# A graph network kernel on one core: relation bias, edge items and layer statistics moved into neighbouring stages, 816 places for attention items instead of 848, extremes by TensorE

## The reference, cut to what matters

```
x = x + relations(layernorm(x))     # sum over edges of (x W[type])[src], by dst, * 0.5**0.5
                                    #   + h_bias + x loop_weight * 0.5**0.5
x = x + experts(layernorm(x))       # edge attention over 8192 places gives the gates: top 2 of 4,
                                    #   softmax; out += gate_e * (gelu(x W1_e + b1_e) W2_e + b2_e)
x = x + neighbours(layernorm(x))    # x W_self + mean over edges of maxk32(x W_neigh)[src], by dst
x = x + slices(layernorm(x))        # 8 heads, 64 slices: softmax of logits, tokens, attention
                                    #   between tokens, back to rows, W_out and b_out
```

## Time and profile before

| what | us |
| --- | --- |
| median of 3 runs | 6084.98 |
| lowest and highest | 6080.4 and 6094.47 |
| the profiled execution, its time | 6074.39 |
| its span | 6072.7 |

### The profile page before, as it was taken

The page is one execution under the profiler, slowest core; times in us unless marked ns, Lnnn a source line. Parts: engine busy times, 40 slices in busy tenths (PEclk is TensorE's granted clock), DMA queues, the critical chain, the costliest instruction groups (busy, mean ns, idle before and its releaser), DMA issues. The chain is left out here.

```text
span 6072.7 us, 74083 instructions
## 1 busy us (share of the span) xinstructions
PE 4259.9 (70%) x18413; PEld 3046.3 (50%) x18414; DVE 2604.2 (43%) x8618; ACT 1712.5 (28%) x3921; POOL 3332.0 (55%) x3370
## 2 busy tenths in 40 slices
PE   5888877645555554467777777756668888888498
PEld 2455446333333333445555555545246666666366
DVE  7655424333333332433333333334944443443682
ACT  3344330000000000123333333325365543443132
POOL 5777665666666665055555555551256666666121
PEclk9999998776667766577878888878889999999698
DMA  6444442433333333122222122216144444443001
GB/s 219 154 158 156 158 155 79 130 92 93 91 92 92 92 96 82 14 70 43 43 41 44 40 44 42 42 34 191 41 147 144 138 121 121 121 121 115 16 1 43
DMA packets 331160, 564.00 MB, mean 93 GB/s; under 512 B 75064, under 2 KB 231365, under 8 KB 324507
## 3 DMA queue, kind: packets, MB, share of 16 engines
q0 software_dynamic: 141088, 319.86, 19.9%
q1 hardware_dynamic: 189789, 240.92, 12.6%
HBM read 461.01 MB, written 99.50 MB: 92 GB/s over the span
## 5 line engine op out<-in xcount | busy, mean ns | idle before, releaser
L990 POOL DMA_INDIRECT e_ring<-table,erow x1040 | 990.1, 952 | 523.4 <-issue 267.2
L1290 PE MATMUL e_sums<-e_ring,e_onehot 128*128 128x257 f32 x2080 | 772.2, 518 | 626.6 <-issue 351.5
L2236 POOL DMA_INDIRECT t_source<-source_rows,t_index x848 | 804.3, 948 | 717.9 <-DVE t_parts L2319 476.5
L1401 POOL DMA_INDIRECT e_ring<-table,esrc x800 | 791.2, 989 | 424.2 <-issue 207.3
L1290 PEld LDWEIGHTS e_sums<-e_ring,e_onehot 128*128 128x128 f32 x2080 | 494.0, 257 | 889.9 <-issue 570.8
L585 POOL DMA_INDIRECT r_ring<-rows,esrc x528 | 584.4, 1107 | 239.8 <-issue 131.8
L2395 PE MATMUL t_out<-t_w,t_hidden 128*128 128x256 f32 x1600 | 526.8, 459 | 172.3 <-issue 166.8
L1477 PE MATMUL e_total<-e_loads,e_times 128*128 128x256 f32 x2176 | 577.4, 397 | 47.7 <-issue 36.9
L2395 PEld LDWEIGHTS t_out<-t_w,t_hidden 128*128 128x128 f32 x1600 | 345.6, 225 | 308.6 <-issue 263.1
L1477 PEld LDWEIGHTS e_total<-e_loads,e_times 128*128 128x128 f32 x2176 | 413.3, 198 | 138.6 <-issue 64.7
L1488 PE MATMUL e_sums<-e_ring,e_onehot 128*128 128x256 f32 x1600 | 432.8, 393 | 48.7 <-DMA e_ring<-table,esrc 31.6
(11 more groups left out here) (447 smaller groups left out, 6371.8 us busy)
## 6 DMA issues: line engine op xcount, KB each, us to landing
table<-r_stage SPq DMA_DIRECT2D x49, 1024.0 KB
e_loads<-table SPq DMA_DIRECT2D x384, 128.0 KB
t_near<-near_rows SPq DMA_DIRECT2D x106, 256.0 KB
m_outputs<-first_outputs SPq DMA_DIRECT2D x49, 512.0 KB, 4.9
first_outputs<-t_stage SPq DMA_DIRECT2D x96, 256.0 KB
e_ring<-table,erow POOLq DMA_INDIRECT x1040
t_source<-source_rows,t_index POOLq DMA_INDIRECT x848
e_ring<-table,esrc POOLq DMA_INDIRECT x800
```

The costliest lines, as they stand in the source:

```text
L990: eng.indirect_dma_start(ring[:, t % BODY, 0:D], None, table, bass.IndirectOffsetOnAxis(ap=b.erow[:, EARLY + t:EARLY + t + 1], axis=0)).th ...
L1290: eng.matmul(sums[g % SUMS][:, 0:ACCW], onehot[t % ONEHOTS][:, :], ring[:, t % BODY, :], start=(t % GROUP == 0), stop=(t % GROUP == GROUP ...
L1401: eng.indirect_dma_start(ring[:, t % BODY, :], None, table, bass.IndirectOffsetOnAxis(ap=b.esrc[:, FROM + t:FROM + t + 1], axis=0)).then_i ...
L2236: eng.indirect_dma_start(source[s][:, q, :], None, a.source_rows, bass.IndirectOffsetOnAxis(ap=index[s][:, q:q + 1], axis=0)).then_inc(gat ...
```

## The change

What it does, function by function:

- **relation_sums** also loads h_bias, by SP ahead of its waits, and DVE adds it to b.x in seven pieces of seven windows (lift), at tiles 520, 528 and so on.
- **add_relations, the second row_statistics and edge_items** are one stage, joined_items. Its DVE code goes between the items' steps and join (b.x += acc * 0.5**0.5 for seven windows) and tally (bn_stats of seven windows).
- **The items are packed**: their edges are counted from a window's first edge, not from a tile's, so an item may begin anywhere in the sorted list. For that the last tile of every window is gathered (edge), the edges in it are counted, the ends and the item counts per window are laid out by a second product and six scan steps, and nine gathers fetch 128 edges from any position (anywhere).
- **attention_inputs**: the extremes over partitions come from a transpose and a product on PE with a DVE maximum between, instead of POOL's reduction; the memset of extra moves here; the store of source_rows increments a.sourced and is not awaited. **far_peaks** keeps one memset and makes the iota only in the wide path; **attention_edges** waits for a.sourced before POOL's first gather.
- **attention_edges**: MAIN is 816, so 102 turns, the last four without dense work and unrolled; b1 and b2 are loaded ahead of the weights, and PE waits for the weights of expert e at its first turn.
- **blend**: PE takes three experts, DVE the fourth (gate) ahead of its addition.
- **sparse_table**: the third statistics are combined at its start; MATCH_REPLACE8 writes TAKEN; the mask of what was taken is made by ACT (hide, seven windows late) and multiplied by POOL (choose).
- **add_neighbours, the fourth row_statistics and slice_weights** are one stage, neighbours_and_weights: ACT scales acc by the share, window by window, DVE joins and counts in runs of seven windows.
- **slice_tokens** writes the softmax rows in a layout by window (f.soft), half of it in the memory of big; **slice_output** multiplies from there without a copy and has four banks.

```diff
-MAIN = -(-(GT * N // GSPACE + NW + 16) // TURN) * TURN
+MAIN = -(-(GT * N // GSPACE + NW // 2 + 10) // TURN) * TURN
...
+TAKEN = -2.0 ** 127
...
+STATED = 7
+def variances(eng, s, b, stats, work):     # the seven combining steps of row_statistics
...
 def relation_sums
+    bias_at = [TILES // 2 + GROUP * j for j in range(RUNS)]
+            eng.dma_start(bias[:, :], m["h_bias"].rearrange("(a d) -> a d", a=1).broadcast_to([P, D])).then_inc(offset, 16)
             eng.wait_ge(keyed, 32)
...
+            def lift(j):
+                eng.wait_ge(restored, 16)
+                eng.wait_ge(offset, 16)
+                eng.tensor_tensor(b.x[:, RUN * j:RUN * (j + 1), :], b.x[:, RUN * j:RUN * (j + 1), :],
+                                  bias[:, :].unsqueeze(1).broadcast_to([P, RUN, D]), ALU.add).then_inc(biased, 1)
...
+                if t in bias_at:
+                    lift(bias_at.index(t))
...
 def attention_inputs
-            eng.dma_start(a.source_rows.rearrange("(w p) c -> p w c", p=P), a.rows[:, :, :]).then_inc(stored, 16)
-            eng.wait_ge(stored, 16)
+            eng.dma_start(a.source_rows.rearrange("(w p) c -> p w c", p=P), a.rows[:, :, :]).then_inc(a.sourced, 16)
...
-            eng.wait_ge(bounded, 1)
-            eng.partition_all_reduce(extremes[:, :], bounds[:, :], P, RMAX).then_inc(reduced, 1)
-            eng.wait_ge(reduced, 1)
+            eng.memset(a.extra[:, :, :], 0.0).then_inc(emptied, 1)
+            eng.wait_ge(emptied, 1)
...
+            eng.wait_ge(bounded, 1)
+            eng.transpose(turned[0][0:2 * HEADS, 0:P], bounds[:, :], b.ident[:, :]).then_inc(reduced, 1)
+            eng.wait_ge(bounded, 2)
+            eng.matmul(turned[1][:, 0:2 * HEADS], b.ones[0:2 * HEADS, :], laid[:, :], start=True, stop=True).then_inc(reduced, 1)
...
 def joined_items (DVE)
+            def join(j):
+                run = b.x[:, RUN * j:RUN * (j + 1), :]
+                eng.scalar_tensor_tensor(run, b.acc[:, RUN * j:RUN * (j + 1), 0:D], 0.5 ** 0.5, run,
+                                         ALU.mult, ALU.add).then_inc(joined, 1)
+            def tally(j):
+                eng.wait_ge(joined, j + 1)
+                for w in range(RUN * j, RUN * (j + 1)):
+                    eng.bn_stats(stats[:, w, :], b.x[:, w, :]).then_inc(tallied, 1)
...
+            eng.tensor_copy(whole[:, :], counted[0:NW, 0:1]).then_inc(bounded, 1)
+            join(0)
+            eng.wait_ge(edged, 16)
...
+            for j in range(EARLIER):
+                join(j + 1)
+                tally(j)
             eng.wait_ge(gathered, 16 * GROUND)
...
+            for j in range(EARLIER, RUNS):
+                if j + 1 < RUNS:
+                    join(j + 1)
+                tally(j)
...
 def attention_edges
+                eng.dma_start(w1[:, e, :, :], m["W1"][e].rearrange("(k p) f -> p k f", p=P)).then_inc(loaded[e], 16)
+                eng.dma_start(w2[:, e, :, :], m["W2"][e].rearrange("(j p) d -> p j d", p=P)).then_inc(loaded[e], 16)
...
+                if first_turn(t, 1):
+                    eng.wait_ge(a.sourced, 16)
+                    eng.sem_inc(cleared, 1)
...
+                if first_turn(u, EXPERTS):
+                    eng.wait_ge(loaded[e], 32)
...
-            eng.wait_ge(loaded, LOADS)
+            eng.wait_ge(offset, 32)
...
 def blend
+    TURNED = EXPERTS - 1
-                for e in range(EXPERTS):
+                for e in range(TURNED):
...
+            def gate(w):
+                eng.wait_ge(fetched[w % SLOTS], 16 * (w // SLOTS + 1))
+                eng.scalar_tensor_tensor(b.x[:, w, :], outputs[w % SLOTS][:, TURNED, :], a.gate[:, w, TURNED:EXPERTS],
+                                         b.x[:, w, :], ALU.mult, ALU.add).then_inc(gated, 1)
...
 def sparse_table
+    LATER = WAYS - 1
...
+            def choose(w):
+                eng.wait_ge(masked, w + 1)
+                wait_if(eng, stored[w % WAYS], 16 * (w // WAYS))
+                eng.tensor_tensor(sparse[w % WAYS][:, :], mask[w % WAYS][:, :], full[w % WAYS][:, 1, :], ALU.mult).then_inc(chosen, 1)
...
-                    eng.scalar_tensor_tensor(sparse[q][:, :], left[q][:, :], LOWEST, full[q][:, 1, :],
-                                             ALU.is_equal, ALU.mult).then_inc(chosen, 1)
+                    eng.sem_inc(searched, 1)
...
+            def hide(w):
+                eng.wait_ge(searched, w + 1)
+                wait_if(eng, chosen, w - WAYS + 1)
+                eng.activation(mask[w % WAYS][:, :], left[w % WAYS][:, :], ACT.Relu, bias=less[:, 0:1],
+                               scale=-2.0 ** -126).then_inc(masked, 1)
...
+                if w >= LATER:
+                    hide(w - LATER)
                 eng.wait_ge(multiplied, w + 1)
...
 def neighbours_and_weights
+            for w in range(NW):
+                eng.activation(b.acc[:, w, 0:D], b.acc[:, w, 0:D], ACT.Copy, scale=share[:, w:w + 1]).then_inc(scaled, 1)
...
+            join(0)
+            for j in range(RUNS):
+                if j + 1 < RUNS:
+                    join(j + 1)
+                count(j)
...
 def slice_output
-                eng.activation(weight[s][:, :, :], f.swt[:, :, bass.ds(w * P, P)], ACT.Copy).then_inc(copied, 1)
+                    mm = eng.matmul(product[w % BANKS][:, 0:D], f.soft(w)[:, q, :], f.outp[:, q, :],
```

More of the change, by code:

```diff
@@ L1986, in edge_items @@
         count = sb("i_count", [P, NW])
-        start = sb("i_start", [P, NW])
+        whole = sb("i_whole", [NW, 1], I32)
+        edge = sb("i_edge", [NW, P], I32)
+        part = sb("i_part", [NW, P])
+        inner = sb("i_inner", [NW, 1])
+        end = sb("i_end", [NW, 1])
+        laid = sb("i_laid", [NW, NW])
+        ends = sb("i_ends", [P, NW + 1])
+        length = sb("i_length", [P, NW], I32)
+        parts = sb("i_parts", [P, NW], I32)
+        excess = sb("i_excess", [P, NW])
+        starts = [sb(f"i_start{s}", [P, NW]) for s in range(2)]
+        weighed = sb("i_weighed", [P, GROUND, NW])
+        first = sb("i_first", [P, GROUND])
         passed = sb("i_passed", [P, GROUND, NW])
@@ L2144, in attention_edges @@
         picked = [ctx.enter_context(nc.psum_tensor(f"t_picked{s}", [P, BANK], F32)) for s in range(2)]
-        loaded = sem("t_loaded")
+        loaded = [sem(f"t_loaded{e}") for e in range(EXPERTS)]
+        offset = sem("t_offset")
         emptied = sem("t_emptied")
@@ L2614, in sparse_table @@
         best = [sb(f"n_best{s}", [P, 8]) for s in range(WAYS)]
+        mask = [sb(f"n_mask{s}", [P, D]) for s in range(WAYS)]
         sparse = [sb(f"n_sparse{s}", [P, D]) for s in range(WAYS)]
+        less = sb("n_less", [P, 1])
+        work = sb("n_work", [P, 4, NW])
+        std = sb("n_std", [P, NW])
+        stated = sem("n_stated")
+        rooted = sem("n_rooted")
+        scaled = sem("n_scaled")
         turned = [ctx.enter_context(nc.psum_tensor(f"n_turned{s}", [P, BANK], F32)) for s in range(2)]
@@ L2755, in _ @@
                                ACT.Copy).then_inc(evacuated, 1)
[L2758 to L2774 removed]
+            for w in range(NW - LATER, NW):
+                hide(w)
 def attention_phase(nc, b, m):
@@ L2849, in _, with join, count @@
             eng.wait_ge(loaded, 192)
+        @block.scalar
+        def _(eng):
+            eng.wait_ge(shared, 1)
+            for w in range(NW):
+                eng.activation(b.acc[:, w, 0:D], b.acc[:, w, 0:D], ACT.Copy, scale=share[:, w:w + 1]).then_inc(scaled, 1)
+            eng.wait_ge(stated, STATED)
+            eng.activation(std[:, :], b.rstd[:, :], ACT.Sqrt).then_inc(rooted, 1)
         @block.vector
         def _(eng):
-            v = Chain(eng, done)
+            def join(j):
+                run = slice(RUN * j, RUN * (j + 1))
+                eng.wait_ge(scaled, RUN * (j + 1))
+                eng.tensor_tensor(b.x[:, run, :], b.x[:, run, :], b.acc[:, run, 0:D], ALU.add).then_inc(added, 1)
+            def count(j):
+                eng.wait_ge(added, j + 1)
+                for w in range(RUN * j, RUN * (j + 1)):
+                    eng.bn_stats(stats[:, w, :], b.x[:, w, :]).then_inc(tallied, 1)
+            v = Chain(eng, done)
+            eng.reciprocal(share[:, :], b.degree[:, :]).then_inc(shared, 1)
+            join(0)
[3 more added lines that the diff above has]
+                count(j)
+            eng.wait_ge(tallied, NW)
+            s = Chain(eng, stated)
+            variances(eng, s, b, stats, work)
             eng.wait_ge(loaded, 192)
```

332 lines of the change are left out of this document (172 added, 160 removed).

## The result

The changed kernel takes 5947.11 us (median of 4 runs, 5926.13 to 5956.54) against 6084.48 us before (4 runs): a ratio of 0.977, 95% interval 0.9753 to 0.9786. The prediction was 5941 us, with a range of 5908 to 5983. Its profiled execution is the slowest of the four, 5956.5 us with a span of 5954.5; the sum had put that execution at 5930.

What follows compares the result with a forecast made beforehand. One core runs a long chain of barrier-separated stages, each with its own bound. The terms sum to -144 us, taking 6074.4 to 5930; plus 10.6 (median above profiled execution) gives 5941 us, range 5908 to 5983.

Steps and rivals of the forecast that it cites:

- B: add_relations, second statistics and edge_items as one stage: 78.9 us become 55, taken as -22 us (bounds -18, -26).
- H: Neighbours, fourth statistics and slice weights in one stage: 79.2 us become 39, taken as -39 us (bounds -36, -41).
- E: attention_edges with 816 places, 102 turns for 106: the last four turns' gathers go, -41 us (bounds -38, -44).
- F: blend, a quarter of PE's products to DVE: DMA becomes the bound, 0 to -11 us, taken as -6.
- C: attention_inputs and far_peaks, extremes on PE and store not awaited: both waits go, -11 us (bounds -3, -12).
- D: attention_edges, weights awaited per expert: PE starts 6 to 7 us in instead of 18.0, -12 us (bounds -7, -14).
- G: Sparse table, third statistics moved in and the mask taken off DVE: -17 us (bounds -12, -21).
- A: Relation sums, bias added by DVE in seven pieces: each may stretch a gather, 0 to +13 us, taken as +5.
- Rival 1: Relation sums and joined items: DVE stops POOL wherever it streams SBUF, 5952 us; it and Rival 2, single, hold 0.2.
- Rival 2: far_peaks: POOL's 8.1 us stay, belonging to the place and not the reduction, 5949 us; with Rival 1, single, 0.2.
- rival 5: attention_edges: the items don't fit in 816, so the far path runs, costing many milliseconds; chance 0.01.
- Rival 4: attention_edges: turns run slower, clock down to about 0.72, each 1.44 us more, eating the 144 us; chance 0.03.

## Why the prediction was right, step by step

The total was 6 us off, but the sum, made against the profiled executions, was 26 us below the profiled one of after (5930 and 5956.5). That one lies 9 us above its median and before's lay 10 below, so up to 19 of the 26 may be the choice of executions. The 6 us of the total are luck in part: attention_edges and the sparse table came out 30 us worse than the sum, blend 6 better, and the total hides the rest because before's median lies above its profiled execution and after's below. The steps:

- **B, H, I, and the mechanisms of E and F held.** B: 57.9 us for 57; the wait for the item gathers was foreseen as 2 to 3 us and is 2.1. H: 38.8 us for 39.
- **C, a right sum for a half right reason.** "I put that on the reduction, the one operation of its kind in this kernel": the runs show the pair of reduction and iota. Without the iota on the path the reduction could have stayed, and the three stages would take some 1.3 us less than with TensorE (69.6 + 4.6 + 4.1 against 70.8 + 4.2 + 4.5), which is the price that the prediction put on TensorE. The awaited store was worth 4.7 us, the gap 8; together they made it -12.6 for -11, just outside the bounds.
- **E was mis-sized**, -41 for -48.7: "the last four, without dense work, are POOL's 32 gathers: 32 x 1.25 = 40.0". The stretch of 41.1 us that I read in the earlier trace rows is one of uneven pairs. On this chip the tail runs at 12 us a turn, since POOL waits for values; where the tail takes 9.7 a turn (38.7 us for four, in the changed kernel on the quicker chip), the 40 would be about right.
- **D failed as a sum**: "PE's later turns are its own: -12 (bounds -7, -14)". Turn 0 did come 7.8 us earlier, but in the run with all weights awaited nothing of it can be seen at the stage's end: the turns behind it gave it back. "100 turns of 14.4 us have PE as their bound" was wrong: PE is busy for 72% of the stage, and the same products take 10.05 us a turn on the other chips. What paces the turns on this chip stays open (see the end). From the values of turn 0 to those of turn 97 it took 1409.5 us after and 1393.2 before; the five profiles of the changed loop on such chips have 1398 to 1421. Whether the loop has become slower by some 15 us or before's one profile was a quick one stays open too; D and E together fell 13.5 us short, and this is all of it.
- **F was mis-sized**, -6 for -12.3: the loads did get the rate of the first slices, 1.50 us a window, not the middle. The better end of the bounds was -11.
- **G is the step that failed.** "The entry saves a barrier and overlaps the statistics with the weights on which PE waits 4 us: -3": it cost 7.2 (from blend's end to the first replacement 19.9 us before and 27.1 after), because it also overlaps them with POOL's memset. I had looked for DVE holding POOL, which was a rival, and not at what POOL does in the stage into which DVE's steps moved. "49 operations ... 49 x 0.355 = -17.3" gave 8.9 from the first replacement to the last: without the waits and increments between the groups it gives 16.0 (the run without DVE's semaphore), and they take back 7.1, some 0.6 us a group, which the operation had covered. So a window took 3.04 us for the 2.94 forecast. The one condition I named, ACT's order, was harmless; the +1 of the last window came.
- **A**, +5 for +2.9, which the variation of the stage covers. The sign was seven gathers over 2 us; all seven were held, four of them to over 2 us. Rival 1, that DVE stops POOL wherever it streams SBUF, held for the forms with two tensors in SBUF, at 1.2 us a gather in A and 1.65 in B, but its price of 11 us didn't come: B lost 3 of its 24 us, where the sum had counted 2, and A is no more than its +5. Rival 2 is out, since the 8.1 us went, and rival 5, since attention_edges has its 816 gathers and no more. Rival 4's lower clock didn't come either: 0.80 over attention_edges against 0.79, at 14.5 us a turn for 14.4.

## What to carry to other kernels

When steps move into another stage, list what the engine that shares their port does there at that moment, in both directions: here a memset of 10.8 us turned three steps of 0.2 us into 10, and one wait took it back. When an operation is taken off the bounding engine, what it covered comes into the open: waits and increments behind it should go to the instruction that is there anyway. And a time that changes with a change is not yet its cause: here it took four runs to see that a pair made the gap, of which the change had removed both halves.

## What was not expected of the hardware

**The same kernel takes 5063 us on one chip and 5947 on another**, with the same instructions and nearly the same busy time of POOL and DVE. attention_edges takes 1035 instead of 1483 us, relation_sums 1325 instead of 1529. The window of attention_edges on the quicker chip, to be read against the third of those after above:

```profile
2279.00:3315.00 1036.00, 894.91 (x6466) 753.01 (x6467) 524.39 (x2347) 449.10 (x805) 777.75 (x815) 0.94 0.29 63
```

PE's clock is 0.94 instead of 0.80 and it is busy for 895 us instead of 1063, which is not the difference of 447. And in the relation sums the quicker chip has the lower clock, 0.65 against 0.70, and is 204 us quicker all the same. In attention_edges there, POOL hardly waits for values (9.1 us), and the turns are its eight gathers, 10.05 us. On the slower chip the waits of the stage are these (us in total, times, longest):

```profile
ACT t_hidden L2304 <- DMA i_keys<-sorted_edges,i_tile: 496.8, 88, 15.2
POOL t_source L2286 <- DVE t_parts L2369: 477.7, 94, 9.8
DVE t_place L2331 <- remote: 433.1, 77, 10.3
...
PEld t_out L2447 <- issue: 250.2, 306, 2.5
...
PE t_out L2447 <- issue: 164.4, 257, 1.5
```

Releasers like a DMA of an earlier stage, "remote" or "issue" are what the profile says when it sees no cause. On the quicker chip the first and the last three of these waits aren't among the eighteen longest, and POOL's for values is the 9.1 us. What holds the engines is open; no run here changed it. The ratio of after to before is the same on both kinds of chip, 0.977 and 0.976.

**An iota behind a reduction over partitions starts about 8 us late.** By the Trainium skill (GPSIMD Engine Reference, section Instruction dispatch) the first call of a freshly loaded kernel pays about 6 us that no instruction shows. The runs agree in kind, with 8 us in which no instruction runs, but ahead of the iota that follows; a memset that followed the reduction started 2.4 us behind it, and the gathers after it at their usual time. That the 8 us are such a load, no run here shows.
